# The second MLP's first tiles issued among the first MLP's last ones, in one block

## What is computed

```python
# first MLP ("m"), 256 -> 1024 -> 256
h  = layer_norm(y, g2, be2)
z  = relu(h @ W1.T + b1) @ W2.T + b2 + h
x1 = x_normalised + layer_norm(z, g3, be3)

# second MLP ("d"), 256 -> 1024 -> 256, with weights as integers and scales per 128 rows
w1 = (fc1_q - 128) * fc1_scales      # two groups of 128 rows
w2 = (fc2_q - 128) * fc2_scales      # eight groups of 128 rows
out = a normalised x1 + 0.5 * (silu(ln(x1) @ w1 + fc1_bias) @ w2 + fc2_bias)
```

## Time and profile before

| | us |
|---|---|
| runs | 2533.41, 2533.52, 2539.47; median 2533.52 |
| profiled execution | 2533.56, of which the span of the trace is 2531.8 |
| PE busy in the span | 2355.1 (93%) |
| DVE, ACT, POOL busy | 1777.8 (70%), 1292.8 (51%), 702.9 (28%) |

### The profile page before, as it was taken

The page is one execution under the profiler, slowest core; times in us unless marked ns, Lnnn a source line. Parts: engine busy times, 40 slices in busy tenths (PEclk is TensorE's granted clock), DMA queues, the critical chain, the costliest instruction groups (busy, mean ns, idle before and its releaser), DMA issues. The chain is left out here.

```text
span 2531.8 us, 43746 instructions
## 1 busy us (share of the span) xinstructions
PE 2355.1 (93%) x16024; PEld 2178.7 (86%) x16024; DVE 1777.8 (70%) x3293; ACT 1292.8 (51%) x2026; POOL 702.9 (28%) x468
## 2 busy tenths in 40 slices
PE   7999995899999969999999999999999997599999
PEld 6888985899999968898898898888999997599998
DVE  5776765899999857466466566565687874877774
ACT  4445443444444325455455455455666663455555
POOL 1111112445444423123123023033343431211110
PEclk9999997999999979999999999987999999799999
DMA  5000000000000000000000000011000010000001
GB/s 180 0 0 0 0 0 20 1 0 0 0 0 1 1 17 1 17 8 8 17 8 8 17 8 8 17 47 38 26 17 25 17 42 12 25 26 25 25 25 34
DMA packets 42971, 45.69 MB, mean 18 GB/s; under 512 B 3088, under 2 KB 41872, under 8 KB 42640
## 3 DMA queue, kind: packets, MB, share of 16 engines
q1 hardware_dynamic: 42896, 44.69, 5.4%
HBM read 27.90 MB, written 16.78 MB: 18 GB/s over the span
## 5 line engine op out<-in xcount | busy, mean ns | idle before, releaser
L1881 DVE TENSOR_TENSOR m_a_lo<-m_a,m_a_hi 128x512 fp32r<-128x512 f32 x128 | 124.3, 986 | 91.5 <-ACT m_a_hi L1840 91.5
L1836 ACT ACTIVATE d_a<-d_ps_wide,d_b,d_w_gain 128x512 f32<-128x512 f32 x128 | 100.0, 782 | 136.8 <-PE d_ps_wide L272 134.8
L1291 POOL TENSOR_TENSOR p_kf<-p_kf,p_k_shift 128x1024 f32<-128x1024 f32 x64 | 119.5, 1903 | 155.5 <-DVE p_k_shift L1426 155.5
L1793 PE MATMUL m_ps_z<-m_w_hi,m_a_hi 128*128 128x256 f32 x512 | 146.2, 286 | 0.0
L1793 PE MATMUL d_ps_z<-d_w_hi,d_a_hi 128*128 128x256 f32 x512 | 143.6, 281 | 0.9 <-DVE d_a_lo L1881 0.9
L1793 PE MATMUL m_ps_z<-m_w_hi,m_a_lo 128*128 128x256 f32 x512 | 144.2, 282 | 0.0
L1793 PE MATMUL m_ps_z<-m_w_lo,m_a_hi 128*128 128x256 f32 x512 | 144.1, 281 | 0.0
L1793 PE MATMUL d_ps_z<-d_w_lo,d_a_hi 128*128 128x256 f32 x512 | 143.4, 280 | 0.0
L1793 PE MATMUL d_ps_z<-d_w_hi,d_a_lo 128*128 128x256 f32 x512 | 142.6, 279 | 0.0
L1881 DVE TENSOR_TENSOR d_a_lo<-d_a,d_a_hi 128x512 fp32r<-128x512 f32 x128 | 85.8, 689 | 76.4 <-ACT d_a_hi L1840 71.9
L1836 ACT ACTIVATE m_a<-m_ps_wide,m_b 128x512 f32<-128x512 f32 x128 | 87.6, 684 | 89.2 <-PE m_ps_wide L272 88.9
(11 more groups left out here) (356 smaller groups left out, 8501.4 us busy)
## 6 DMA issues: line engine op xcount, KB each, us to landing
residual<-in_x SPq DMA_DIRECT2D x8, 1024.0 KB, 11.9
attn<-p_attn SPq DMA_DIRECT2D x32, 256.0 KB, 2.2
m_attn<-attn SPq DMA_DIRECT2D x16, 512.0 KB, 3.8
out<-residual SPq DMA_DIRECT2D x16, 512.0 KB, 2.9
raw_weights<-in_d_q SPq DMA_DIRECT2D x2, 1024.0 KB, 7.2
d_scale<-in_d_scale SPq DMA_DIRECT2D x2, 1024.0 KB, 5.6
raw_weights<-in_m_w1T SPq DMA_DIRECT2D x1, 1024.0 KB, 4.8
raw_weights<-in_m_w2T SPq DMA_DIRECT2D x1, 1024.0 KB, 8.0
```

Source lines behind the costliest of these rows:

```text
L1291: pool.tensor_tensor(f, f, k_shift[:, i, :].unsqueeze(2).broadcast_to([P, HEADS, M]), ALU.subtract).then_inc(k_shifted, 1)
L1793: mm = pe.matmul(z, a, w[:, f, :], start=(f == 0 and k == 0 and j % 2 == 0), stop=(f == FC - 1 and k == 2), skip_group_check=True)
L1836: act.activation(self.a[f % RING][:, :], self.ps_wide[f % 2][:, :], self.func, bias=self.b1[:, f:f + 1], scale=gain(f))
L1881: dve.tensor_tensor(self.a2[1][:, f, :], self.a[f % RING][:, :], self.a2[0][:, f, :].bitcast(F32), ALU.subtract).then_inc(self.a_lo, 1)
```

## The change

Both MLPs become one block. `Pipeline` gets its phases in groups (eight on PE and ACT, five on DVE, two on POOL), and a function `cross` runs four steps, 17 to 20, in which each group of the first MLP's step s is followed by the same group of the second MLP's step s - 17. The second MLP counts its tiles on (16 to 31) and uses the first one's buffers for n, h, a, the PSUM banks and their semaphores; its weights lie where raw weights, attention rows and the first MLP's w1 lay. Its `unit` is inverted in eight pieces of 128 columns, two at the end of each of DVE's steps 4 to 7. The other weights are made by calls (hooks) behind given groups of steps 17 to 19, w2 in two halves. The first MLP's last tile (15) leaves out `take_z`, `roots_o`, `normalise_o`, `gain_o` and `update_x` at their usual places: DVE's `take_z` comes at the end of step 19, the others in steps 20 and 21.

```diff
+def cross(ending, beginning, turn, hooks={}):
+    for s in range(turn, turn + CROSSED):
+        for g in range(len(ending.groups)):
+            ending.group(g, s)
+            beginning.group(g, s - turn)
+            if (s, g) in hooks:
+                hooks[s, g]()
+    beginning.run(begin=CROSSED)
...
+        self.next.load_vectors(sync)
+        Pipeline(sync, NM, [[(0, load)]]).run(begin=3)
         sync.wait_ge(self.mlp.w_lo, 2)
         self.raw.load_q(sync, self.dram)
+        self.next.load_scales(sync)
+        self.next.store(sync)
...
+            self.steps = Pipeline(dve, NM, [[(wide, mlp.split_a(dve, 0, 1)), (1, add_attn)],
+                                            [(wide, mlp.split_a(dve, 2)), (mlp.N, mlp.split_h(dve))],
+                                            [(wide, mlp.split_a(dve, 3)), (mlp.Z + 1, all_but_last(NM, update_x))],
+                                            [(wide, mlp.split_a(dve, 4)), (mlp.Z, all_but_last(NM, take_z))],
+                                            [(wide, mlp.split_a(dve, 5, 6, 7))]],
+                                  between={4 + k: lambda k=k: self.next.invert_units(2 * k, 2 * k + 1) for k in range(UNITS // 2)})
...
+            hooks = self.next.hooks()
+            hooks[TURN + 2, 4] = self.take_last
+            self.next.steps.between[CROSSED] = self.update_last
+            cross(self.steps, self.next.steps, TURN, hooks)
...
+    def load_scales(self, sync):
+        before, dram, half = self.before, self.before.dram, FC // 2
+        sync.wait_ge(before.y_added, NM)
+        sync.dma_start(self.scale1, dram["d_scale1"][1].partition_broadcast(P)).then_inc(self.scale1_loaded, 16)
+        sync.dma_start(self.scale2, dram["d_scale2"][0:half].partition_broadcast(P)).then_inc(self.scale2_loaded, 16)
+        sync.dma_start(self.b2, dram["d_b2"].partition_broadcast(P)).then_inc(self.b2_loaded, 16)
+        sync.wait_ge(self.mlp.w2_made, 1)
+        sync.dma_start(self.scale2, dram["d_scale2"][half:FC].partition_broadcast(P)).then_inc(self.scale2_loaded, 16)
...
+            self.steps = Pipeline(dve, NM, [[(wide, mlp.split_a(dve, 0, 1)), (0, statistics)],
+                                            [(wide, mlp.split_a(dve, 2)), (0, normalise)],
+                                            [(wide, mlp.split_a(dve, 3)), (mlp.N, mlp.split_h(dve))],
+                                            [(wide, mlp.split_a(dve, 4)), (mlp.Z, take_z)],
+                                            [(wide, mlp.split_a(dve, 5, 6, 7))]], between={})
...
+            return {(TURN, 0): first, (TURN, 2): lambda: self.dequantise_w2(0), (TURN, 4): second,
+                    (TURN + 1, 1): lambda: self.dequantise_w2(1), (TURN + 2, 0): lambda: self.low_w2(0),
+                    (TURN + 2, 2): lambda: self.low_w2(1)}
...
+            act.wait_ge(layer.mlp.w2_made, k + 1)
+            act.wait_ge(layer.mlp.wide_done, FC * NM)
+            act.activation(layer.mlp.narrow_weights[0][:, at, :], layer.q2[:, at, :], ACT.Copy).then_inc(layer.mlp.w2_hi, 1)
...
+            return {(TURN, 5): self.high_w1, (TURN + 1, FC - 1): lambda: self.act.wait_ge(self.layer.gain_step, 3),
+                    (TURN + 2, 1): lambda: self.high_w2(0), (TURN + 2, 3): lambda: self.high_w2(1)}
```

More of the change, by code:

```diff
@@ L6 @@
+import math
 from contextlib import ExitStack
@@ L772, in run, with all_but_last, phase @@
                     run(i * unroll + (first + k - lag), (k - lag) % unroll)
-        for s in range(end, turns + depth):
+        for s in range(last, turns + self.depth if end is None else end):
             self.step(s)
+def cross(ending, beginning, turn, hooks={}):
[6 more added lines that the diff above has]
+    beginning.run(begin=CROSSED)
+def all_but_last(turns, run):
+    def phase(t, s):
+        if not (isinstance(t, int) and t == turns - 1):
+            run(t, s)
+    return phase
 def pipeline(eng, turns, phases, unroll=2, between={}):
-    Pipeline(eng, turns, phases, unroll, between).run()
+    Pipeline(eng, turns, [phases], unroll, between).run()
 def fp4_layer(core, dram, weights, performer_raw):
@@ L2077, in rest @@
         def rest(self):
-            self.steps.run(begin=3)
+            self.steps.run(begin=3, end=TURN)
+            hooks = self.next.hooks()
+            hooks[TURN + 2, 4] = self.take_last
+            self.next.steps.between[CROSSED] = self.update_last
+            cross(self.steps, self.next.steps, TURN, hooks)
     class Scalar:
@@ L2138, in rest @@
         def rest(self):
-            self.steps.run(begin=3)
+            self.steps.run(begin=3, end=TURN)
+            following = self.layer.next.Scalar(self.layer.next, self.act)
+            hooks = following.hooks()
+            hooks[TURN + 3, 5] = self.normalise_last
+            cross(self.steps, following.steps, TURN, hooks)
     class Tensor:
@@ new lines, in rest, with name_weight_sems, await_wide, await_narrow @@
+            self.steps.run(begin=3, end=TURN)
+            cross(self.steps, self.layer.next.mlp.tensor(self.pe), TURN)
+class WholeWideMlp(Mlp):
+    def name_weight_sems(self):
+        sem = self.core.sem
+        self.whole_ready, self.w1_made, self.w1_hi, self.w1_lo = (sem(f"d_{e}") for e in ("whole_ready", "w1_made", "w1_hi", "w1_lo"))
+        self.w2_made, self.w2_hi, self.w2_lo = (sem(f"d_w2_{e}") for e in ("made", "hi", "lo"))
+        self.loaded = sem("d_loaded")
+    def await_wide(self, pe):
+        pe.wait_ge(self.whole_ready, 1)
+        pe.wait_ge(self.w1_lo, 1)
+    def await_narrow(self, pe, f):
+        if f % (FC // 2) == 0:
+            pe.wait_ge(self.w2_lo, f // (FC // 2) + 1)
+    def await_scale(self, act):
+        act.wait_ge(self.loaded, 16 * 4)
```

449 lines of the change are left out of this document (260 added, 189 removed).

## The result

The changed kernel takes 2503.71 us (median of 2502.95, 2503.42, 2504.00 and 2511.11) against 2534.64 on the same chip: a ratio of 0.9881, 95% interval 0.9858 to 0.9904. On the profiled execution of before that is 2503.4, and 2490 was forecast: the sign is right, the gain is 30 us where 43 were expected. The profiled execution after is the one of 2511.11 (span 2509.4). It starts its MLPs at 1728.40, 7.8 us later than the profiled execution of before at 1720.63, in a part that the change doesn't touch. The forecast for it was 811.2 - 46.3 + 3.0 = 767.9. The question is where 13.1 us went.

A forecast was written before the change was run, and what follows sets the result against it. PE was taken as the bound inside each MLP, with DVE next and the change of blocks as the gap. 2533.56 - 46.3 + 2.0 (tile 15) + 1.0 (margins) = 2490.3, rounded to 2490; range 2487 to 2498.

The forecast's parts named there:

- The removed gap: Between the two MLPs' last tiles: 46.3 us lost in PE's waits and the half clock behind them would all come back.
- No mechanism I see goes lower: Floor of the whole kernel's time: 2487.3 us, with all of the gap's 46.3 us recovered.
- The inversions in steps 4 to 7: On DVE, two pieces per step, some 3.5 us a pair, covered by 4.8 free; costed at 0, without cover 14.
- 21.41 us a tile: PE's steady pace in the second MLP, from the earlier trace; sixteen tiles need 342.6 us without a wait.
- The stall for tile 15: Ahead of chunk 1: `take_z` of tile 13 slips 4.4 us, delaying `normalise_o` and chunk 7; PE waits 2.0 us.
- four thin margins: Tile 15's chunk 7, step 19's `split_h`, w2's low halves before `narrow` 0 and 4: 1 us together, bounds 0 and 8.
- The table load: On ACT before chunk 0's Silu: 1.30 us, PE waits for nothing; by the skill's page PE would wait 1.3.
- The last tile's end and the transfers: `take_last` ending step 19 is off the path, and vector and scale loads land in time: costed at 0.
- Rival 1: DVE bounds the crossing through stretched `normalise` and missed margins; PE waits 6 to 14 us, 2493.5 to 2501.5; chance 0.22.
- the one long wait: In w2's chain over three engines before `narrow` 0, a third or more of the gap stays: 2502 to 2526; chance 0.06.
- the fall of the clock: In the crossing, small waits bring the clock to 0.50; 2583 us if all four steps ran so; chance 0.03.

The follow-up runs named there:

- x5: Changed kernel with inversions between splits of chunks 6 and 7, weights allocated first, third tile's statistics earlier, first half of w2 later; 2492.09 us, ratio 0.9824.
- x12: x5 with weights placed as in x9, first w2 half behind step 17's chunk 7, second half moved, last tile's `normalise_o` two chunks later; 2489.03 us, ratio 0.9802.
- x1: Changed kernel with the inversions of steps 4 to 7 moved between the splits of chunks 6 and 7; 2502.02 us, ratio 0.9858.
- x3: Changed kernel with the first MLP's weights allocated ahead of its small arrays; 2503.21 us, ratio 0.9861.
- x4: Changed kernel with the second MLP's third tile's statistics done at the end of step 18; 2504.29 us, ratio 0.9865.
- x7: Changed kernel with the first MLP's last tile finished at its usual place, not deferred; 2512.86 us, ratio 0.9908.
- x9: Changed kernel with 96 bytes free ahead of the first MLP's weights and 32 behind (start 32 over 128); 2496.59 us, ratio 0.9854.
- x10: Changed kernel with 64 bytes free on either side of the first MLP's weights (start 0 over 128); 2503.13 us, ratio 0.9876.

## Why the prediction was wrong, point by point

- **The removed gap, 46.3.** Right to 1 or 2 us. PE has no wait above 1.6 us from step 4 on, the clock stays at 1.00, and x5 with 765.8 comes within a microsecond of 811.2 - 46.3 = 764.9; its second MLP's faster pace (16 tiles of 21.32) gives 1.4 there and its waits take as much. "No mechanism I see goes lower" is wrong by what x12 has below that, 3.1, from the pace of the weights' place.
- **The inversions in steps 4 to 7, costed at 0.** This is the step that failed most: 5.8 us by the four intervals, 5.7 by x1. The pair's estimate of 3.5 was right for a DVE that is not held up (3.75 in x1), but the bound of 0.68 for each small instruction fell: one took 2.38. The cover was read wrongly: 4.8 us were free in a step as a sum, but behind chunk 7 POOL starts two instructions of 2.4 us, and DVE's idle time stood elsewhere, ahead of chunk 7. The doubling beside POOL was in the rows that I used for `normalise` (3.46 against 1.38) and I did not apply it here.
- **21.41 us a tile, taken over from before.** The second step that failed: 21.58, and 25.25 for 25.14. The number of matmuls is the same, and I took their speed to be the same; the moved allocation was not costed at all. Undoing it (x3) gives 4.5 us.
- **The stall for tile 15, 2.0.** The mechanism is right, the size half. `take_z` of tile 13 stands 15.98 us behind `turn_n`, 4.3 later than the 11.72 of the earlier trace rows (forecast 4.4):
```profile
2119.72 1.22 DVE L2115 TENSOR_TENSOR m_o<-m_ps_z,m_b 128x1024 f32<-128x1024 f32 x1
```
```profile
2125.06 1.10 ACT L2200 ACTIVATE m_o<-m_o,m_o_shift,m_o_rstd 128x256 f32<-128x256 f32 x2 [4.50 <-POOL m_o_shift L2075]
...
2126.63 0.67 ACT L1911 ACTIVATE m_a_hi<-m_ps_wide,m_b 128x512 fp32r<-128x512 f32 x1
```
  `normalise_o` stands 5.34 behind `take_z`, where 5.86 was taken from the earlier trace rows, and chunk 7 ends 2.24 later as forecast. The wait is 1.0.
- **1 us for the four thin margins.** Mis-sized: 2.0 by the waits of step 19, and 3.2 by x4, in which the wait of step 20 shrinks too. The stretched `normalise` was in the sum for step 19 (3.46 of the 5.17, measured 3.45). What it had wrong is the start: the first chunk is ready 6.2 us into the step (at 2157.54, with the first `widen` at 2151.34), not 4.3, since ACT comes to the table load only at 2154.80, behind `normalise_o` and chunk 7 of tile 15. From there to the end of `split_h` DVE takes 16.4 us, where 1.5 + 15.4 were forecast, so it ends at 22.7 and not at 21.2 of 21.4.
- **The table load at no cost.** Right. It starts at 2154.80, where the instruction ahead of it ends, and the Silu behind it at 2156.09, 1.29 later (1.30), and PE waits for nothing there:
```profile
2154.80 1.28 ACT L1907 ACT_TABLE_LOAD   x1
2156.09 0.78 ACT L1907 ACTIVATE m_a<-m_ps_wide,d_b,d_w_gain 128x512 f32<-128x512 f32 x1
```
  The further drain that the Trainium skill counts with it (ScalarE: Activation LUTs, What ACT_TABLE_LOAD costs) is not to be seen in these rows.
- **The last tile's end and the transfers, at 0.** Right for the transfers: no wait of PE or DVE in the crossing is for one. The last tile's end costs the 0.7 of step 20, through `gain_o`; x7 shows that the deferral still saves 7.2 us.
- **The rivals.** Rival 1 had the right engine for the crossing, but not the place: in steps 17 and 18 `normalise` took 1.38 both times, not 3.46, and most of what was lost lies outside the crossing, in steps 4 to 7 and in the pace. Neither the one long wait nor the fall of the clock came in after; x7, which differs only in where the last tile's end stands, has a wait of 8.0 us and the clock at 0.50 behind it. Both failed steps were terms that I set to 0 or left out, so no rival priced them and the range ended below the result.
- **The sum.** Of the 13.1 us, the inversions are 5.7 and the pace some 4.4; steps 19 and 20 cost some 2 more than the 1.0 put on them, and tile 15's stall 1.0 less than its 2.0. That is 11; the other 2 are not accounted for.

## What to carry to other kernels

Work that is moved under another engine's cover has to be placed at the point of the step where its own engine waits and where POOL runs no long instruction: a sum of free time per step does not show either, a timeline of both engines over one step does. When a change moves allocations, compare the steady pace per tile of stretches that the change should not touch; less than one per cent there, over many tiles, cost nearly as much here (4.5 us) as the inversions (5.7). A phase that waits on a chain over three engines should stand behind, not ahead of, the work that the bounding engine needs next.

## What the runs showed of the hardware

- The pace of matmuls that wait for nothing depends on where their operands lie in SBUF: moving the weights by 32 bytes (x9 against x10) changed a tile of the second MLP from 21.14 to 21.57 us, 2%, all of it in the matmuls that read w2. Over all runs it lay between 21.14 and 21.73. The place is not all: in x12 tiles of the first MLP take 24.91 and later ones 24.96 to 25.28 at the same addresses.
- The hold-up between DVE and POOL goes both ways, and the one that starts later can be held until the other ends: a DVE instruction of 0.29 us took 2.38 beside one of POOL, and a POOL instruction of 0.20 took 0.85 beside one of DVE. Some instructions with one operand are held up as well (a copy of 512 columns took 2.62 for 0.42), others not (a reciprocal of 128 columns kept its 0.95). POOL's root on 128x4 held nothing up in x1.
- Waits of 1.34 us in 7 did not lower the granted clock; one of 8.0 us in x7 did, to 0.50 in 2178 to 2181; in 2184 to 2200 it was 1.00 again.
